# Layer 2's key and value projections moved into the combination stage; value rows kept on chip

## What is computed

```python
# layer 1, attention: queries from normed x, keys and values from the context
q = split(query @ wq.T + bq);  k = split(key @ wk.T + bk);  v = split(value @ wv.T + bv)
x = softmax(mask(q k^T / 4)) v                    # 16 heads of 16
return x @ wo.T + bo
...
# layer 2, attention: the same context, other maps, no bias
qh = split(q @ q_map);  kh = split(k @ k_map);  vh = split(k @ v_map)
merged = (softmax(qh kh^T / 4) vh) merged over heads
return merged @ output_map
```

## Time and profile before

| what | us |
|---|---|
| median of 3 runs | 1966.49 (1964.01 to 1973.61) |
| the profiled execution | 1959.69, span 1957.7 |
| project, 23 to 247 | 224 |
| attention of layer 1, to its last result, 247 to 616 | 369 |
| combine, 1298 to 1429 | 131 |
| attention of layer 2, 1429 to 1796 | 367 |

### The profile page before, as it was taken

How to read it: one execution, slowest core, us unless ns; L and a number is a source line. 1 busy time by engine, 2 the same in 40 slices (tenths; PEclk the granted TensorE clock), 3 DMA queues, 4 the chain that set the end, 5 groups by cost and what they waited for, 6 DMA issues and landing times. The chain is left out here.

```text
span 1957.7 us, 30459 instructions
## 1 busy us (share of the span) xinstructions
PE 1556.4 (80%) x11926; PEld 1038.4 (53%) x11927; DVE 1298.3 (66%) x2050; ACT 923.4 (47%) x1235; POOL 722.2 (37%) x931
## 2 busy tenths in 40 slices
PE   2877359999996862989999999936649999996624
PEld 2766223333332762989999999932213333332422
DVE  2544269999993547565555555449669999994557
ACT  1333218888885211434444444411118888886104
POOL 0112015655550411443333333233115455450556
PEclk6988759999998865999999999967759999998765
DMA  7566556655551521122212221124355655561002
GB/s 224 175 201 196 179 85 142 138 130 139 132 130 38 215 87 56 36 84 90 87 49 88 90 89 44 39 76 150 107 104 129 140 136 134 131 138 47 1 0 86
DMA packets 125823, 212.47 MB, mean 109 GB/s; under 512 B 28512, under 2 KB 70432, under 8 KB 124528
## 3 DMA queue, kind: packets, MB, share of 16 engines
q1 hardware_dynamic: 90800, 119.25, 20.9%
q0 software_dynamic: 34880, 91.28, 18.6%
HBM read 122.61 MB, written 86.79 MB: 107 GB/s over the span
## 5 line engine op out<-in xcount | busy, mean ns | idle before, releaser
L882 DVE TENSOR_REDUCE a_nmax<-a_ring 128x2 f32<-128x1024 f32 x512 | 608.6, 1219 | 40.1 <-PE a_ring L793 39.9
L865 ACT ACTIVATE a_pexp<-a_ring 128x1024 f32<-128x1024 f32 x512 | 522.4, 1026 | 207.3 <-PE a_ring L803 207.2
L817 PE MATMUL a_pout<-a_pexp,a_v 128*17 128x256 f32 x4096 | 321.1, 386 | 0.7 <-ACT a_pexp L865 0.7
L793 PE MATMUL a_ring<-a_k,a_q 64*128 64x512 f32 x1024 | 244.5, 475 | 79.8 <-DMA a_q<-qs 69.7
L803 PE MATMUL a_ring<-a_q,a_k 64*128 64x512 f32 x1024 | 259.1, 502 | 7.8 <-DMA a_q<-a_nT 4.1
L1458 ACT ACTIVATE e_full<-e_pH,b1T 128x256 f32<-128x256 f32 x320 | 133.5, 468 | 271.3 <-PE e_pH L1418 271.3
L1487 DVE TENSOR_TENSOR e_hid_lo<-e_full,e_hid_hi 128x512 fp32r<-128x512 f32 x160 | 128.2, 805 | 151.6 <-ACT e_hid_hi L1466 151.6
L803 PEld LDWEIGHTS a_ring<-a_q,a_k 64*128 64x128 f32 x1024 | 96.6, 185 | 230.2 <-DVE a_nmax L882 134.7
L1437 PE MATMUL e_pY<-fc_w_hi,e_hid_hi 128*128 128x256 f32 x640 | 185.0, 289 | 9.0 <-DVE e_hid_lo L1487 9.0
L1418 PE MATMUL e_pH<-e_rowsT_hi,fc_w1T_hi 128*128 128x256 f32 x640 | 182.3, 285 | 1.5 <-DVE e_rowsT_lo L1333 1.5
L793 PEld LDWEIGHTS a_ring<-a_k,a_q 64*128 64x128 f32 x1024 | 99.9, 192 | 156.5 <-DMA a_q<-qs 71.3
(11 more groups left out here) (279 smaller groups left out, 2595.4 us busy)
## 6 DMA issues: line engine op xcount, KB each, us to landing
outs<-a_osb SPq DMA_DIRECT2D x64, 256.0 KB, 3.2
fc_raw<-in_L_ffn_fc_w SPq DMA_DIRECT2D x16, 1024.0 KB, 7.3
a_k<-ks POOLq DMA_DIRECT2D x112, 128.0 KB, 3.4
a_q<-qs POOLq DMA_DIRECT2D x112, 128.0 KB, 3.6
vs<-p_va SPq DMA_DIRECT2D x16, 544.0 KB, 10.2
a_v<-vs POOLq DMA_DIRECT2D x16, 544.0 KB, 5.2
ks<-p_parts_k_hi SPq DMA_DIRECT2D x32, 256.0 KB
ks<-p_parts_k_lo SPq DMA_DIRECT2D x32, 256.0 KB
```

The lines of the kernel that those rows point to most:

```text
L793: mm = e.matmul(max_bank(m)[:, hh, :], q[j][at, p, t * P:(t + 1) * P], k[j][at, p, :], start=True, stop=True)
L817: mm = e.matmul(pout[n % 2][32 * h:32 * h + VW, at], v[b % 2][:, t, g * HG + h, :], pexp[t][:, h, at], start=(t == 0 and half == 0), stop= ...
L865: e.activation(pexp[t][:, 2 * p:2 * p + 2, :], score_bank(n * U + i)[:, :, :], ACT.Exp).then_inc(exped, 1)
L882: e.tensor_reduce(nmax[n % 2][:, :].rearrange("p (x y t) -> p x y t", x=2, y=2)[:, :, p, t], max_bank(m)[:, :, :], AX.X, ALU.max, negate=T ...
```

## The change

- **project** makes k0, v0 and q0 alone. The context and the tokens get PSUM buffers of their own (pC, pH), and the products take turns in two (pJ). The low parts of k0 and q0 are cut by GpSimd, no longer by VectorE. v0 is copied by ScalarE from PSUM into `S.values.rows`, an SBUF tensor for all 8 batches with the column of ones set once; nothing is stored to vs. SyncE issues k0 of batch b, then q0 of batch b-1.
- **bias of the values**: bv is multiplied by wo in setup (two matmuls of a widened column vector) and added to bo, since the weights of a softmax sum to one.
- **attention** reads its values from that tensor; the 16 loads and their waits are gone.
- **combine** gets the context again (one DMA of 512 KB a batch by GpSimd, 4 MB in all), transposes it (pC), ScalarE copies it and cuts the high part, GpSimd the low part; TensorE makes k1 and v1 in one PSUM buffer (pK) one after the other; ScalarE copies k1, cuts its high part, copies v1 to its place; GpSimd cuts the low part of k1; SyncE stores k1 behind the queries. The buffers acc and r become one.
- The buffers of the division after attention are allocated in route and merge, not in attention. No instruction changes by that.

```diff
 
+class Values:
+
+
+    def __init__(self, S, l):
+        self.ctx = ExitStack()
+        self.rows = self.ctx.enter_context(S.nc.sbuf_tensor(f"values{l}", [P, NT, H, VW], F32))
+
+    def of(self, b):
+        return self.rows[:, b * TPB:(b + 1) * TPB, :, 0:DH]
+
+    def count_column(self, e):
+        return e.memset(self.rows[:, :, :, DH:VW], 1.0)
+
...
+class Projection:
+
...
+    def cut_high(self, e, b, evictions):
+        e.wait_ge(self.taken, (b + 1) * evictions)
+        if b:
+            e.wait_ge(self.stored, 64 * b)
+        e.activation(self.parts[HI][:, :, :], self.full[:, :, :], ACT.Copy).then_inc(self.high, 1)
+
+    def cut_low(self, e, b):
+        e.wait_ge(self.high, b + 1)
+        e.tensor_tensor(self.parts[LO][:, :, :], self.full[:, :, :], self.parts[HI][:, :, :], ALU.subtract).then_inc(self.low, 1)
+
+    def store(self, e, b):
+        e.wait_ge(self.low, b + 1)
+        store_parts(e, self.dst, b, self.parts, self.stored)
...
             @block.sync
             def _(e):
                 for b in range(B):
-                    for j, by in (("q0", 1), ("k0", 0), ("v0", 0), ("k1", 0), ("v1", 0)):
-                        store(e, j, b - by)
-                store(e, "q0", B - 1)
-                for j in ("v0", "v1"):
-                    e.wait_ge(kst[j], 16 * B)
-                for j in jobs:
-                    e.wait_ge(kst[j], 64 * B)
+                    k0.store(e, b)
+                    if b:
+                        q0.store(e, b - 1)
+                q0.store(e, B - 1)
+                for job in (k0, q0):
+                    e.wait_ge(job.stored, 64 * B)
 
...
                 for b in range(B):
-                    e.wait_ge(tpl, 2 * b + 1)
-                    product("k0", b, cT)
-                    turn_tokens(b)
-                    values("v0", b, cT)
-                    product("k1", b, cT)
-                    values("v1", b, cT)
+                    e.wait_ge(low_c, b + 1)
+                    if b:
+                        e.wait_ge(v_taken, b)
+                    project_heads(e, k0_bank(b), w["k0"], cT).then_inc(k0.done, 1)
+                    if b:
+                        e.wait_ge(q0.taken, b * KD)
+                    project_values(e, v0_bank(b), w["v0"], cT).then_inc(v_done, 1)
                     if b + 1 < B:
                         turn_context(b + 1)
-                    e.wait_ge(tpl, 2 * b + 2)
-                    product("q0", b, hT)
+                    e.wait_ge(low_h, b + 1)
+                    e.wait_ge(k0.taken, (b + 1) * KD)
+                    project_heads(e, q0_bank(b), w["q0"], hT).then_inc(q0.done, 1)
+                    if b + 1 < B:
+                        turn_tokens(b + 1)
...
                 for b in range(B):
                     if b + 2 < B:
-                        e.wait_ge(turned, 2 * b + 1)
+                        e.wait_ge(turned_c, b + 1)
                         load_context(S, e, b + 2, ld_c[b % 2])
                     if b + 1 < B:
                         nb.power(e, b + 1, 0)
-                    e.wait_ge(cuth["k1"], b + 1)
-                    if b:
-                        e.wait_ge(kst["k1"], 64 * b)
-                    e.tensor_tensor(parts["k1"][LO][:, :, :], full["k1"][:, :, :], parts["k1"][HI][:, :, :],
-                                    ALU.subtract).then_inc(cutl["k1"], 1)
+                    k0.cut_low(e, b)
+                    q0.cut_low(e, b)
...
                 for b in range(B):
-                    high_turned(2 * b + 1, hT, "q0")
-                    high("k0", b)
-                    e.wait_ge(pj["k1"], b + 1)
+                    high_tokens(b)
+                    k0.cut_high(e, b, KD)
+                    e.wait_ge(v_done, b + 1)
+                    if b + 1 < B:
+                        high_context(b + 1)
+                    e.activation(values.of(b), by_head(as_tokens(v0_bank(b))), ACT.Copy).then_inc(v_taken, 1)
+                    e.wait_ge(q0.done, b + 1)
                     if b:
-                        e.wait_ge(cutl["k1"], b)
-                    e.activation(full["k1"][:, :, :], bank("k1", b)[:, :, :], ACT.Copy).then_inc(ev["k1"], 1)
-                    high("k1", b)
-                    e.wait_ge(pj["v1"], b + 1)
-                    if b:
-                        e.wait_ge(kst["v1"], 16 * b)
-                    e.activation(va[1][:, :, :, 0:DH], tokens_bank("v1", b).rearrange("p t (h c) -> p t h c", h=H),
-                                 ACT.Copy).then_inc(ev["v1"], 1)
-                    if b + 1 < B:
-                        high_turned(2 * b + 2, cT, "v1")
-                    e.wait_ge(pj["q0"], b + 1)
-                    if b:
-                        e.wait_ge(cutl["q0"], b)
+                        e.wait_ge(q0.low, b)
                     for t in range(KD):
-                        e.activation(full["q0"][:, t, :], bank("q0", b)[:, t, :], ACT.Identity,
-                                     bias=bq4[:, t:t + 1]).then_inc(ev["q0"], 1)
-                    high("q0", b)
+                        e.activation(q0.full[:, t, :], q0_bank(b)[:, t, :], ACT.Identity, bias=bq4[:, t:t + 1]).then_inc(q0.taken, 1)
+                    q0.cut_high(e, b, KD)
...
                 for b in range(B):
+                    low_tokens(b)
                     e.wait_ge(mke, b + 1)
-                    e.wait_ge(pj["k0"], b + 1)
+                    e.wait_ge(k0.done, b + 1)
                     if b:
-                        e.wait_ge(cutl["k0"], b)
+                        e.wait_ge(k0.low, b)
...
                     if b + 1 < B:
-                        prepare(b + 1)
-                        low_turned(2 * b + 2, cT)
+                        stats(b + 1)
+                        mask(b + 1)
+                        low_context(b + 1)
                         apply(b + 1)
-                    low("q0", b)
...
+                def load_context(b):
+                    if b >= 2:
+                        e.wait_ge(turned_c, b - 1)
+                    e.dma_start(context[b % 2][:, :, :], S.a["ctx_1024"][b, :, :].rearrange("(t p) c -> p t c", p=P)
+                                ).then_inc(ld_c[b % 2], 16)
+
+                def low_context(b):
+                    e.wait_ge(high_c, b + 1)
+                    e.tensor_tensor(cT[b % 2][LO][:, :, :], whole_c[:, :, :], cT[b % 2][HI][:, :, :], ALU.subtract
+                                    ).then_inc(low_c, 1)
+
+                load_context(0)
                 load_rows(0)
+                load_context(1)
                 load_rows(1)
-                @rounds(e, 0, 2)
-                def _(i, j, k):
+                values.count_column(e).then_inc(counted, 1)
+                for n, j in enumerate(raw):
+                    e.wait_ge(whi, n + 1)
+                    e.tensor_tensor(w[j][LO], raw[j][:, :, :], w[j][HI], ALU.subtract).then_inc(wlo, 1)
+                for i in range(B):
                     nb1.power(e, i, 0)
-                    if inside(i + 2):
+                    if i + 2 < B:
                         load_rows(i + 2)
-                    nb2.power(e, i, j)
+                    low_context(i)
+                    nb2.power(e, i, i % 2)
+                    if i + 2 < B:
+                        load_context(i + 2)
+                    if i:
+                        k1.cut_low(e, i - 1)
+                k1.cut_low(e, B - 1)
...
+                turn_context(0)
+                e.wait_ge(wlo, 2)
                 @loop(e, B)
                 def _(b):
+                    e.wait_ge(low_c, b + 1)
+                    if b:
+                        e.wait_ge(v_taken, b)
+                    project_heads(e, pK, w["k1"], cT[b % 2]).then_inc(k1.done, 1)
+                    if b + 1 < B:
+                        turn_context(b + 1)
+                    e.wait_ge(k1.taken, b + 1)
+                    project_values(e, pK, w["v1"], cT[b % 2]).then_inc(v_done, 1)
...
+                def take_context(b):
+                    e.wait_ge(turned_c, b + 1)
+                    if b:
+                        e.wait_ge(low_c, b)
+                    e.activation(whole_c[:, :, :], pC[:, :, :], ACT.Copy).then_inc(whole, 1)
+                    if b >= 2:
+                        e.wait_ge(v_done, b - 1)
+                    e.wait_ge(whole, b + 1)
+                    e.activation(cT[b % 2][HI][:, :, :], whole_c[:, :, :], ACT.Copy).then_inc(high_c, 1)
+
+                for j in raw:
+                    e.activation(w[j][HI], raw[j][:, :, :], ACT.Copy).then_inc(whi, 1)
+                take_context(0)
                 @loop(e, B)
                 def _(b):
+                    e.wait_ge(k1.done, b + 1)
+                    if b:
+                        e.wait_ge(k1.low, b)
+                    e.activation(k1.full[:, :, :], pK[:, :, :], ACT.Copy).then_inc(k1.taken, 1)
+                    k1.cut_high(e, b, 1)
+                    if b + 1 < B:
+                        take_context(b + 1)
```

(8 more changed lines are left out.)

252 lines of the change are left out of this document (127 added, 125 removed).

## The result

| what | before | after |
|---|---|---|
| median of the runs, us | 1967.76 (4 runs) | 2068.27 (2066.92 to 2068.93, 4 runs) |
| the profiled execution, us | 1959.69 | 2066.92 |
| attention of layer 1 starts (its first memset on GpSimd) | 247.2 | 229.0 |
| low part of layer 2's queries, first and last | 1334.1, 1418.6 | 1327.2, 1520.5 |
| attention of layer 2, its last memset | 1431.3 | 1538.5 |

The ratio is 1.0507 with a 95% interval of 1.048 to 1.0534: 5% slower, 100 us in the medians and 107 in the two profiled executions. The prediction was 2085 (2018 to 2128): right in sign and in the mechanism that costs the time, 17 us too high.

A forecast was written before the change was run, and what follows sets the result against it. The prediction took key and query stores, on half the DMA engines, to fill project and VectorE to bound combine. It summed 1959.7 - 5.0 (project) + 127.9 (combine) = 2082.6 and said 2085 us, range 2018 to 2128.

The forecast's parts named there:

- Attention at zero: Both attentions: only loads and one wait leave them, so costed at nothing, with a range of 0 to -2 us.
- Half of the engines for keys and queries: Project and combine: key and query stores share the same eight of 16 DMA engines, at 134 to 178 GB/s.
- full overlap: Rival, project and combine: two stores overlap fully, L = 11.5, +62.9 us, 2023; chance 10%.
- The ring of project: Project: the next q0 high cut waits for the last-issued q0 store; rounds of 25.7 us, stage -5.0 us.
- the gap of T+10.2: Project: from T, the landing of q0's store, 10.2 us pass until the next two jobs are stored.
- L: Project and combine: time for two store jobs issued one behind the other to land, taken as 15.5 us.
- The ring of combine: Combine: k1's high cut waits for k1's store, issued behind the queries; turns of 29.9 us, not 12.6; stage +127.9.
- The start of combine: Combine: the first low part of the queries ends at 1336.2 instead of 1334.1, behind the context's added work.
- The sum: Whole kernel: 1959.7 - 5.0 (project) + 127.9 (combine) = 2082.6 us by the profiled execution, stated as 2085.
- the deeper one: Rival: store rate stays at 134 GB/s or below, or expert rows collide; L 18.5 or more, 2128 and above; 7%.
- only combine's ring closes: Rival: project runs by bytes, -68 us, while combine still costs +128; 2020; chance 6%.
- the faster one: Rival: project and combine keep their stores hidden, project -68, combine +4 us; 1896; chance 6%.

The follow-up runs named there:

- before_s16: Kernel before with queries' and keys' DRAM layout as part, head, row: stores go to 128 rows, not 8 heads; attention loads 14 times a group; 1886.4 us (0.9584).
- after_s16: Kernel after with queries' and keys' DRAM layout as part, head, row: stores go to 128 rows, not 8 heads; attention loads 14 times a group; 1985.5 us (1.009).
- all_first: Kernel after; SyncE stores q0 ahead of k0 in project, k1 ahead of queries in combine; GpSimd cuts k1's low part ahead of the context's; 1902.8 us.
- vec_behind: all_first with combine's two low cuts (k1, context) moved from GpSimd to VectorE, behind the low part of the queries; 1899.4 us (0.9661).
- no_cuts: all_first with GpSimd in combine filling the low parts of k1 and the context with zeros instead of cutting them; 1892.1 us (0.9629).

## Why the prediction was right, step by step

- **Attention at zero**: right. From memset to division layer 1 takes 375.3 against 375.7 us, and from layer 2's last memset to the first product of the last stage 481.8 against 481.4.
- **Half of the engines for keys and queries**: right, and now shown by before_s16 and after_s16, where in project and combine nothing but the shape of the store changed (the attentions' loads changed with it) and the rate of the stores alone went from 195 to 315 GB/s. The trace of before had shown only that the share was one half; that the shape was the cause came from the Trainium skill (DMA: Bandwidth & Descriptors, "Why a DMA increments its semaphore by 16 and not by 1"), and the runs agree with it. Its rule reads the slowest dimension of both sides; here the first dimension of the destination (8) decided. The prediction says that other engines for keys than for queries would give its second rival; it is the first in its list, full overlap.
- **The ring of project**: the first store at 48.9 and the second round's at 61.6 were to be about 50 and 62, the gap of T+10.2 held to within 0.1 us and shrank to T+6.9 when its one slow link was changed. **L** was the term that was mis-sized: 13.7 us instead of 15.5. Seven landings at 1.8 make 12.6, and project came out 18.2 shorter instead of 5.0. The step that failed is the rate: I took the row with 159 GB/s, where stores were queued behind others; two jobs alone go as the row with 178 says (14.3), a little better (195 GB/s in the window above). The nearest row was that of combine, where the queries are alone, as two jobs between two gaps are.
- **The ring of combine**: gaps of 14.4 measured four times, then 13.5, 13.3 and 10.8, against 14.4, 13.6, 13.5 and 11.3. L was 13.5, or 13.9 to 14.9 in the turns in which expert rows are loaded too. From the first to the last of the queries' low parts that is 193.3 us where the prediction's terms give 204.5, and 84.5 before: +108.8 for +120.
- **The start of combine** failed the other way: the first low part was to end at 1336.2, 0.9 us later than before; measured from the stage's own start it came 11.3 later. I had priced the low cuts on GpSimd at their own 2.35 us and nothing on VectorE. In these rows of after, VectorE stands while GpSimd subtracts: its four stretched groups and a subtraction beside each.

```profile
1283.53 3.49 DVE L1629 SCALAR_TENSOR_TENSOR c_acc<-c_yg,gate,BIG 128x256 f32<-128x256 f32 x4 [14.97 <-DMA c_yg<-ytok]
1284.46 1.48 POOL L1604 TENSOR_TENSOR c_w_v_lo<-wv,c_w_v_hi 128x512 fp32r<-128x512 f32 x1
...
1292.51 5.31 DVE L1653 SCALAR_TENSOR_TENSOR X<-c_acc,c_rstd,X 128x256 f32<-128x256 f32 x4 [0.22 <-POOL c_rstd L353]
...
1293.99 2.35 POOL L1594 TENSOR_TENSOR c_cT_lo<-c_whole_c,c_cT_hi 128x1024 fp32r<-128x1024 f32 x1
...
1306.43 4.93 DVE L361 TENSOR_SCALAR c_hn<-X,c_mv,c_rstd 128x256 f32<-128x256 f32 x4
...
1308.20 2.35 POOL L1594 TENSOR_TENSOR c_cT_lo<-c_whole_c,c_cT_hi 128x1024 fp32r<-128x1024 f32 x1
...
1316.38 4.35 DVE L1629 SCALAR_TENSOR_TENSOR c_acc<-c_yg,gate,c_acc 128x256 f32<-128x256 f32 x4
...
1317.30 2.35 POOL L394 TENSOR_TENSOR c_parts_k_lo<-c_full_k,c_parts_k_hi 128x1024 fp32r<-128x1024 f32 x1
```

  The same groups took 1.67, 1.67, 1.45 and 1.67 us before, so these four are 11.6 us longer, and from the first of them to the first low part it is 43.7 us instead of 32.0, 11.6 more. That is the whole late start. The prediction's sign for VectorE, 100 us busy in about 255, failed by the same term: it was 127 in 256, for 296 instructions against 297 before.
- **The sum**: -18.2 in project, +11.3 for combine's late start, +108.8 for its turns, +5.3 behind the last, +0.4 in attention: 107.6 for 107.2 measured between the two profiled executions. The prediction had -5.0, +0.9, +120, +7.0 and nothing, 122.9. The errors in L (13 in project, 11 in combine's turns, 2 behind the last) had one sign, the start had the other (10). So combine's 125.4 for 127.9 is in good part luck: it would have come out 13 us short with the start as forecast. The last step was not clean either: 2082.6 and the 7 us between the profiled execution and the median make 2089.6, not 2085.
- **The rivals**: full overlap (L = 11.5) and the deeper one (18.5) are out by L = 13.7 to 14.9; that only combine's ring closes is out by project's waits; the faster one names the right condition, that the awaited store must not be the last one issued, and all_first meets it: 1902.8, where that rival was put at 1896.

## What to carry to other kernels

Where a single buffer is reused after its store, ask of the store that is awaited what was issued in front of it and what can be issued while it flies: if it is the last of its round, its whole landing is added to every round, whatever the bytes say. An engine that produces for an in-order queue has to produce in that queue's order; a ready result behind a later one costs as much as a slow one. Before moving work to relieve a transfer, look at the shape of the transfer: the share of busy engines with only this kind in flight (0.5 here) told of a gain for which no moving of work was needed, 81 us in before_s16.

## What the runs showed of the hardware that I had not expected

- GpSimd's subtraction of two SBUF tensors (128x1024, 2.35 us) stops VectorE while it runs: in after a group of four that takes 1.45 to 1.67 us alone took 3.3 to 5.3 beside it, and in all_first a single instruction of 0.4 us lasted 6.3 beside two of them. In vec_behind, where GpSimd cuts nothing but the weights, no group but the first is stretched. Not every kind suffers: in after the mean of one `c_hn` is 977 ns against 419 before, of the second `c_acc` 564 against 480, but the statistics of one input stay at 414 against 413, and the queries' low part, which reads one side from PSUM, at 1218 against 1214. GpSimd itself loses little (2.34 to 2.62).
- The Trainium skill ("SBUF — State Buffer", "SBUF: two separate sides") says this: the two engines share a port pair that one instruction holds alone to its end, and VectorE needs it in its two-port modes, or for two SBUF inputs if GpSimd's instruction reads SBUF. The rows agree on all four kinds, if `c_hn`, which has one tensor input, runs in such a mode. No row names the mode, but no_cuts speaks for it: of the groups beside fills, which read nothing, the one of `c_hn` was stretched to 4.08 us, and the eight with two inputs kept their 1.64 to 1.67. On one point the rows and the skill don't meet. The Trainium skill (the same section) gives the pair to the instruction that starts first. Here VectorE's is recorded first (1292.51, a single instruction of 4.12 us) and GpSimd's subtraction 1.5 us later, behind its issues of loads, and it is VectorE that stands. The same issues in before (1309.15) stretched nothing. The runs leave open why VectorE stands from then on.
- TensorE's granted clock was 0.80 in project before, 0.79 after, and 0.90 in before_s16, with 1.00 from 62 to 172, where TensorE had hardly waited. Its 800 matmuls of the stage took 130 us of busy time instead of 143. A stage that is freed of a wait can so gain more than the wait.
